# Layer 3's state scan and router rewritten: a partition per channel and state, B in PSUM, router arithmetic on ScalarE, sums in column tiles

## What is computed

```python
delta = softplus(x @ W_delta.T)                    # 256 x 128 for each block
B_sel, C_sel = x @ W_B.T, x @ W_C.T                # 16 states
def step(h, (d_t, x_t, b_t, c_t)):                 # h: 128 channels x 16 states
    decay = exp(d_t[:, :, None] * A)
    h = h * decay + (d_t * x_t)[:, :, None] * b_t[:, None, :]
    return h, einsum('bdn,bn->bd', h, c_t)
out = layernorm(scan(step)) @ W_ctx.T * context_scale

topk_vals, topk_idx = top_k(x @ router_w + router_b, 2)
gates = softmax(of the two values, 0 elsewhere)
routed = sum over 8 experts of gates * (silu(x @ w1) * (x @ w3)) @ w2; shared experts likewise, ungated
```

## Time and profile before

| | us |
|---|---|
| median of 3 executions | 2742.13 (2737.71 to 2745.82) |
| profiled execution | 2738.4 |
| its span, first to last instruction | 2737.1 |
| busy: TensorE / VectorE / ScalarE / GpSimd | 2218.0 / 1987.8 / 1401.9 / 819.3 |
| first state scan of layer 3 starts at | 2303.93 |

### The profile page before, as it was taken

One profiled execution on the slowest core, in us unless ns is written; L12 is line 12 of the kernel. 1 busy time (PEld: TensorE's weight loads), 2 busy tenths in 40 slices (PEclk: granted clock), 3 DMA queues, 4 the chain that ended last, 5 costly groups with the idle time before them and its releaser, 6 DMA issues.

```text
span 2737.1 us, 46943 instructions
## 1 busy us (share of the span) xinstructions
PE 2218.0 (81%) x17922; PEld 1564.0 (57%) x18077; DVE 1987.8 (73%) x4099; ACT 1401.9 (51%) x3576; POOL 819.3 (30%) x460
## 2 busy tenths in 40 slices
...
GB/s 79 18 183 190 174 197 176 182 183 181 178 196 227 291 86 1 1 1 1 1 1 2 1 1 1 22 13 23 31 21 8 6 26 124 143 169 164 172 175 115
DMA packets 108863, 257.78 MB, mean 94 GB/s; under 512 B 11744, under 2 KB 49888, under 8 KB 108128
## 3 DMA queue, kind: packets, MB, share of 16 engines
...
## 4 chain that ended last, share of the span: by engine, by line
PE 49%; DVE 22%; ACT 12%; issue 8%; DMA 7%; SPq 1%; POOL 0%; another core or an unknown queue 0%; POOLq 0%; DVEq 0%; ACTq 0%
DMA h<-dtu_rows 6%; PE psum L324 3%; PE psum L683 3%; DVE h L1487 3%; PE psum L679 3%; PE psum L490 3%; ACT pr L1831 3%; PE psum L731 3%; PE psum L570 3%; ACT dA L1783 2%; PE psum L615 2%; PE psum L401 2%; PE psum L690 2%; PE psum L428 2%; ACT pt L1875 2%
## 5 line engine op out<-in xcount | busy, mean ns | idle before, releaser
L2074 POOL TENSOR_TENSOR h<-h,Crep 128x1024 f32<-128x1024 f32 x128 | 322.4, 2520 | 566.7 <-DVE h L1487 566.7
L2058 POOL TENSOR_TENSOR pr<-pr,rsum 128x512 f32<-128x512 f32 x192 | 236.0, 1236 | 547.0 <-DVE rsum L1368 547.0
L1487 DVE TENSOR_TENSOR_SCAN h<-dA,h 128x1024 f32<-128x1024 f32 x128 | 305.0, 2385 | 16.8 <-ACT dA L1971 16.7
L1402 DVE TENSOR_REDUCE mx<-psum 128x4 f32<-128x1024 f32 (+1 forms) x192 | 230.2, 1216 | 106.5 <-PE psum L688 106.5
L1875 ACT ACTIVATE pt<-psum 128x1024 f32<-128x1024 f32 x192 | 189.0, 1020 | 143.8 <-PE psum L690 143.7
L1971 ACT ACTIVATE dA<-dA,A 128x255 f32<-128x255 f32 x512 | 215.7, 499 | 74.9 <-DMA dA<-delta_rows 74.5
L2108 POOL TENSOR_TENSOR h<-h,Crep 128x1024 f32<-128x1024 f32 x64 | 179.7, 2809 | 220.0 <-DVE h L1293 219.7
L1831 ACT ACTIVATE pr<-psum,nb 128x256 f32<-128x256 f32 (+1 forms) x512 | 210.5, 429 | 15.5 <-DVE nb L1360 14.5
L1841 ACT ACTIVATE prT<-psum 128x512 f32<-128x512 f32 x192 | 116.1, 604 | 148.7 <-PE psum L584 146.7
L1480 DVE TENSOR_TENSOR h<-h,psum 128x1024 f32<-128x1024 f32 x128 | 153.1, 1208 | 43.0 <-DMA h<-dtu_rows 42.8
L490 PE MATMUL psum<-h,pack_wf 128*128 128x256 f32 x512 | 162.8, 474 | 15.9 <-POOL h L2108 15.9
...
...
## 6 DMA issues: line engine op xcount, KB each, us to landing
dA<-delta_rows SPq DMA_DIRECT2D x128, 512.0 KB, 8.1
h<-dtu_rows SPq DMA_DIRECT2D x128, 512.0 KB, 8.7
Brep<-bc_rows SPq DMA_DIRECT2D x64, 512.0 KB, 4.1
Crep<-bc_rows SPq DMA_DIRECT2D x64, 512.0 KB, 5.5
...
dtu_rows<-dtu SPq DMA_DIRECT2D x64, 64.0 KB, 1.7
...
```

Of the source, the lines that this page charges most:

```text
L1402: ve.e.tensor_reduce(mx[:, qb, 2 * h:2 * h + 2, groups[0]:groups[-1] + 1], k.psum[:, base:base + 2, :].rearrange("p i (n x) -> p i n x", n ...
L1487: ve.e.tensor_tensor_scan(flat(h), flat(k.dA[n % NDA]), flat(h), 0.0, ALU.mult, ALU.add).then_inc(*k.set("scanned", 0, n))
L2058: po.e.tensor_tensor(p3, p3, bcast(k.rsum[n][:, 0:len(heads[r])], P * (q + 1), 2), ALU.mult).then_inc(*k.set("normed", 1, b, p, r))
L2074: po.e.tensor_tensor(h[:, :, :], h[:, :, :], bcast(k.Crep[b % 2][:, :], 4, 1), ALU.mult).then_inc(*k.set("hC", 0, n))
```

## The change

In layer 3 a partition becomes one channel and one state: 8 channels x 16 states, and a group holds 32 channels as four segments of 256 steps. `delta` and `dtu` are stored to HBM (eight stores a block, `stored_rows`) and read back for each group into `dA` (five buffers) and `h` (six), by `read_rows`, with a copy for each of the 16 states: again eight reads of 512 KB a block. ScalarE takes the exponentials in place. B and C come from TensorE already spread over the partitions (weights repeated 8 times, 128 columns, in bank 6); B is read there by VectorE's product, C is copied to SBUF by ScalarE and broadcast along the segments on GpSimd. The sums are four matmuls of a group onto 32 rows each, placed side by side in the array. Bank 6 was a bank of the experts' matmuls, which now share bank 5. The router's division becomes exp(-ln(1+e)) on ScalarE, and a gated one-hot row is one instruction with two scalar operands (compare, multiply), four of 128x8 a block; TensorE sums the two rows of a token while it transposes. `ORDER[3]` is new, and SP's stream is merged from it too. The load stage zeroes one more HBM tensor. At the core of the diff:

```diff
@@ pe_pre3
-        i = pe.e.transpose(bk[0:E3, q * P:(q + 1) * P], k.gt[b % 2][:, q, :], w["ident"])
+        for r in range(2):
+            i = pe.e.matmul(bk[0:E3, q * P:(q + 1) * P], k.gt[b % 2][:, r, q, :], w["ident"], start=r == 0, stop=r == 1)
@@ pe_inner3
-    pe.e.matmul(bk[0:2 * NS, 0:L], w["w_bc3"], xnT[:, :], start=True, stop=True)
-    pe.e.matmul(bk[:, L:2 * L], w["w_delta"], xnT[:, :], start=True, stop=True).then_inc(*k.set("dt", 3, b))
+    pe.e.matmul(bk[:, 0:L], w["w_delta"], xnT[:, :], start=True, stop=True).then_inc(*k.set("dt", 3, b))
     k.pre_read = ("delta", 3, b)
+    yield
+    bc = k.bank[BC_BANK]
+    pe.wait_ge(*k.at("xnT", 3, b))
+    if b:
+        pe.wait_ge(*k.at("dbu", 3, 4 * b - 1))
+    pe.e.matmul(bc[:, 0:L], w["w_brep3"], xnT[:, :], start=True, stop=True)
+    pe.e.matmul(bc[:, L:2 * L], w["w_crep3"], xnT[:, :], start=True, stop=True).then_inc(*k.set("bcrep", b))
@@ pe_states3
-        for n in range(NG):
-            i = pe.e.matmul(bk, k.w["ident"], k.h[g][:, n, :], start=g == 0 and n == 0, stop=g == 3 and n == NG - 1)
+        for s in range(4):
+            i = pe.e.matmul(bk[32 * s:32 * s + 32, 0:L], w["pick"][:, g, :], k.h[n % NH][:, s, :], start=g == 0, stop=g == 3,
+                            tile_position=(0, 32 * s), skip_group_check=True)
@@ ve_pre3
-    ve.e.tensor_scalar(k.g2[:, :, 0], k.g2[:, :, 1], 1.0, None, ALU.add).then_inc(*ve.step())
...
-    ve.e.reciprocal(k.g2[:, :, 0], k.g2[:, :, 0]).then_inc(*ve.step())
...
-    for r, dst in ((0, gt), (1, k.gt2)):
-        ve.e.tensor_tensor(dst[:, :, :], bcast(w["iota8"], QT, 1), bcast(k.rf[:, :, r], E3, 2), ALU.is_equal).then_inc(*ve.step())
...
+    for r in range(2):
+        for q in range(QT):
+            i = ve.e.tensor_scalar(k.gt[b % 2][:, r, q, :], k.w["iota8"], k.rf[:, q, r:r + 1], k.g2[:, q, r:r + 1], ALU.is_equal, ALU.mult)
@@ ve_inner3
-    ve.e.tensor_copy(k.bcrow[b % 2][:, :], bk[0:2 * NS, 0:L]).then_inc(*k.set("crow", 3, b))
@@ ve_states3
-            ve.e.tensor_tensor(h[:, :, :], bcast(k.dtu[x % 2][:, :], NG, 1), k.Brep[n][:, :, :], ALU.mult).then_inc(*k.set("dbu", 3, x, n))
+            ve.wait_ge(*k.at(f"h_in{x % NH}", 3, x))
+            ve.wait_ge(*k.at("bc_copied", x // 4))
+            ve.e.tensor_tensor(h[:, :, :], h[:, :, :], bcast(k.bank[BC_BANK][:, 0:L], 4, 1), ALU.mult).then_inc(*k.set("dbu", 3, x))
@@ ac_pre3
-    ac.e.activation(k.g2[:, :, 1], k.g2[:, :, 1], ACT.Exp).then_inc(*k.set("gate_exp", 3, b))
+    for q in range(QT):
+        i = ac.e.activation(k.g2[:, q, 1:2], k.m8[:, q, 0:1], ACT.Exp, bias=k.m8[:, q, 1:2], scale=-1.0)
...
+    ac.e.activation(k.g2[:, :, 0], k.g2[:, :, 1], ACT.Ln, bias=1.0).then_inc(*ac.step())
...
+    ac.e.activation(k.g2[:, :, 0], k.g2[:, :, 0], ACT.Exp, scale=-1.0).then_inc(*ac.step())
@@ ac_inner3
+    ac.e.activation(k.Crep[b % 2][:, :], k.bank[BC_BANK][:, L:2 * L], ACT.Copy).then_inc(*k.set("bc_copied", b))
@@ ac_states3
-            i = ac.e.activation(k.dA[g][:, n, 1:], k.delta[x % 2][:, 1:], ACT.Exp, scale=k.A3[:, g * NG + n:g * NG + n + 1])
+            i = ac.e.activation(dA[:, s, 1:], dA[:, s, 1:], ACT.Exp, scale=k.A3[:, n % 4, s:s + 1])
@@ sp_store3, sp_reads3 (in place of sp_spread3)
+    stored_rows(k, 3, b, "delta", k.delta3_rows, k.delta[b % 2], 1)
...
+    stored_rows(k, 3, b, "dtu", k.dtu3_rows, k.dtu[b % 2], 0)
...
+            sp.e.dma_start(flat(k.dA[n % NDA]), read_rows(k, k.delta3_rows, x, 0, j)).then_inc(*k.set(f"dA_in{n % NDA}", 3, n, by=16))
...
+            sp.e.dma_start(flat(k.h[n % NH]), read_rows(k, k.dtu3_rows, x, 0, j)).then_inc(*k.set(f"h_in{n % NH}", 3, n, by=16))
```

More of the change, by code:

```diff
@@ L2267, in place_common, with sp_out3 @@
+def sp_out3(k, b):
+    yield
+    k.sp.wait_ge(*k.at("x_ssm", b))
+    k.sp.e.dma_start(k.out.rearrange("(t p) d -> p t d", p=P)[:, b * QT:(b + 1) * QT, :], x_of(k, b)).then_inc(*k.set("stored", by=16))
 def place_common(k, l):
```

230 lines of the change are left out of this document (112 added, 118 removed).

## The result

The changed kernel takes 2696.75 us (median of 4 runs, 2694.34 to 2699.86) against 2740.35 us of the kernel before beside it: a ratio of 0.9845, 95% interval 0.983 to 0.9859. It is 1.55% faster; the forecast was 2694. The profiled execution has a span of 2692.9 us (before 2737.1).

What follows compares the result with a forecast made beforehand. A layer 3 turn was taken as VectorE's work plus one wait on a clogged TensorE; 14 turns -42, drain -7, load +1 give -48 us against 2738.4, about 2694 on the median's scale, range 2668 to 2730 (narrower 2684 to 2706).

Steps and rivals of the forecast that it cites:

- The sum: Whole kernel: -42 us from 14 turns, -7 in the drain, +1 for the load's zero store, -48 in all.
- the lock: Port pair shared by VectorE and GpSimd, held for a whole instruction; the later one is blocked.
- B in PSUM: VectorE's four state products in layer 3 read B from PSUM: 1.208 us against 1.271, -0.25 us a turn.
- rival a: Layer 3's clamp loses the race to GpSimd's product: 2.15 us a turn come back, 2723 us; chance 0.20.
- my walk: Layer 3 turn timed from its last scan: clamp's input ready at 4.5 us, VectorE there at 5.4, 0.9 to spare.
- from 22.7 busy to about 16.7: TensorE's busy time per layer 3 turn: tiled state sums take off 7.7 us, copies and gate records add about 1.7.
- my signs: Signs of being right included TensorE near 70% busy in layer 3 and state sums at 0.6 us a group.
- the wait of the SSM add: VectorE's last SSM-branch add waits 2.6 us a turn on TensorE in layer 3; forecast to go.
- the clamp's hand-over: Layer 3 turn: 0.5 us charged for handing over the clamp's input, or a wait like it.
- rival c: Layer 3 reads come late: 2732 us at 8.7 us landing, 2757 at 10.5; chance 0.12.
- rival of packing (b): VectorE packs nearly perfectly in layer 3, since TensorE has 7 us free: 22.6 us a turn, 2674 us; chance 0.10.
- The head and the drain: Layer 3 before its first scan: 0, bounds -2 and +4 us; after the last turns: 50.3 to 43 us, -7.

Runs made afterwards that it cites:

- the run with the fillers and the moved gate operations: Changed kernel with small unread TensorE matmuls in three places and VectorE's four gate operations moved behind group 3's scan and the next product: 2693.43 us, ratio 0.985.
- three-filler run: Changed kernel with small unread TensorE matmuls ahead of xn's transposes (9), the router's matmul (12), B and C copies (18): 2681.26 us, ratio 0.9812.

## Why the prediction was right, point by point

**The sum.** From the second scan of block 0 to that of block 14 the kernel after goes from the first of these rows to the second:

```profile
2310.90 2.28 DVE L1289 TENSOR_TENSOR_SCAN h<-dA,h 128x1024 f32<-128x1024 f32 x1
...
2647.00 2.28 DVE L1289 TENSOR_TENSOR_SCAN h<-dA,h 128x1024 f32<-128x1024 f32 x1
```

That is 336.1 us against 376.5, 14 turns of 24.0 against 26.9: -40.4 where -42 was forecast. What lies ahead is 0.6 later (forecast +1, for the zero store, which does not show at the start of the trace: VectorE's first instruction is at 17.31 in place of 17.58), what lies behind is 45.9 us against 50.3, -4.4 (forecast -7). Together -44.2, against -48.

**VectorE's work: right in the sum, off in two terms that cancel.** Forecast 22.1, measured 22.06 a turn. The four gate operations cost 0.87 us, not 0.55 (0.28 a record). The gathered adds were to be blocked for 0.55 and aren't: the MoE add ahead of them waits for w2 until just when GpSimd ends. The clamp is at 0.27 (forecast 0.29) and the products at 1.206 (1.208). About 0.2 us more were not taken apart.

I had written that the whole would fall if the small scalar operations took the lock too. They do take it, as the run with the fillers and the moved gate operations shows; they are spared by their place, 0.1 us behind GpSimd's end (2492.01):

```profile
2489.64 2.37 POOL L2118 TENSOR_TENSOR h<-h,Crep 128x1024 f32<-128x1024 f32 x1 [2.06 <-DVE h L1289]
...
2492.11 0.87 DVE L1259 TENSOR_SCALAR gt<-pack_wf,rf,g 128x8 f32<-128x8 f32 x4
```

In all 64 records of the changed kernel the longest takes 0.290 us. That they are never caught was not foreseen, and is luck.

**B in PSUM: right as a term, far too small as a value.** I priced it by two record lengths, at -0.25 us a turn, and the record is as short as forecast. But undone in the finished kernel it costs 4.9 us a turn. The prediction had the exclusion, and the row that shows its other side (GpSimd's 3.25 in the drain), but asked of it only what happens to the clamp. With the product behind the clamp, a product from SBUF would have been blocked four times a turn.

**The clamp (rival a, 0.20).** Rightly judged to win, with less to spare than the 0.9 us of my walk: its exponential (at 2475.99, 0.38 long) is ready 0.55 us before the clamp starts at 2476.92. 1.7 us of exponentials ahead of it were enough to lose all. Priced at 2.15 us a turn, it is worth 3.3.

**TensorE: the step that failed** is "from 22.7 busy to about 16.7", where 19.9 was measured. It was worked out from records at full clock. In the three-filler run, TensorE's work without the fillers is (264.56 - 68.83)/12.5 turns = 15.7 us, so the count of work was good; what I left out is that TensorE, with 7 us of work less, waits more in short pieces and is granted less clock, 0.80 in place of 0.88. So two of my signs failed: TensorE is 83% busy in these turns and not 70%, and a group of sums takes 0.88 us and not 0.6. The sum also had no wait for x_w3 or w2, and these are 1.3 us a turn ahead of L1332 and L1343. With the three fillers they are 0.2, so most of them hang on the low stretch. What counts is which matmuls lie in it and not its length, since turns at 0.86 and at 0.78 are equally long. That x_w3's two halves now share one bank (the other went to B and C) stands behind the wait of L1332 as well; this was not tried apart.

These waits took the place of the 0.5 that I had put down for the clamp's hand-over, which is 0, and of the 0.9 for reads and jitter: 24.05 against 23.9. The forecast of the turn was near for a reason that it didn't have, and that is luck; the 2.9 us won come from what it named, VectorE's shorter work and the wait of the SSM add that goes.

**The reads (rival c, 0.12).** The wait on them is small, as forecast, 0.5 us in twelve turns, but not for the reason given: the landing takes 5.5 us at least and 6.5 in the median, not 4 to 4.5, and the read of h for group 3 is issued 5.9 us before its product, so that there is next to no slack where I had 1.5 us or more. One read more ahead of it costs 1.6 us a turn.

**The router.** Alone it brings nothing in the kernel before; in the finished kernel it is worth 0.5 us a turn in one execution and about 1 by the ratios.

**No rival of packing (b).** 22.6 a turn wasn't reached; even with the clock mended it is 23.1.

**The head and the drain.** Layer 3 starts 1.7 us earlier in this execution, for which no run gives a reason, and its second scan comes 2.4 us later within it, inside the bounds. The drain was taken too low by 2.9 us: its last scans are blocked as before the change, as here, where GpSimd runs until 2669.69:

```profile
2667.33 2.36 POOL L2118 TENSOR_TENSOR h<-h,Crep 128x1024 f32<-128x1024 f32 x1 [3.86 <-DVE h L1289]
2668.80 3.03 DVE L1289 TENSOR_TENSOR_SCAN h<-dA,h 128x1024 f32<-128x1024 f32 x1
```
